# Pairwise products of a recommender head: left operands turned by multiples of 32 rows, so that one buffer of turned rows serves up to seven units

## The reference

```
score_k = exp((x @ w_a + b_a) @ w_b)           # two heads, (w1,b1,w2) and (w3,b3,w4)
q_k     = sum_n x[:, n] * softmax(masked score_k)[:, n]
h       = concat(q1, q2) @ w5 + b5             # 1024 x 300
f6      = h @ w6 + b6
iu, ju  = triu_indices(300, k=1)               # 44850 pairs
cross   = h[:, iu] * h[:, ju] * (v @ v.T)[iu, ju]
f7      = cross @ w7 + b7                      # w7 is 44850 x 300
out8    = concat(f6, f7) @ w8 + b8
out     = einsum('bu,bku->bk', out8, label)    # 1024 x 200
```

## Time and profile before

| | before |
|---|---|
| median of 3 runs | 2047.17 us (2040.95 to 2052.43) |
| profiled execution | 2043.87 us, span 2041.7 us |
| mean granted TensorE clock | 0.934 |
| TensorE busy | 1760.3 us, 86% |
| VectorE busy | 1455.3 us, 71% |
| ScalarE busy | 863.3 us, 42% |
| DMA moved | 629.75 MB, mean 308 GB/s |
| first unit starts | 164.3 us |
| phases 1, 2, 3 start (unit 0) | 588, 1033, 1482 us |
| last unit ends, tail starts | 1868.5 us |

### The profile page before, as it was taken

One profiled execution on the slowest core, in us unless ns is written; L12 is line 12 of the kernel. 1 busy time (PEld: TensorE's weight loads), 2 busy tenths in 40 slices (PEclk: granted clock), 3 DMA queues, 4 the chain that ended last, 5 costly groups with the idle time before them and its releaser, 6 DMA issues.

```text
span 2041.7 us, 23493 instructions
## 1 busy us (share of the span) xinstructions
PE 1760.3 (86%) x6820; PEld 1290.3 (63%) x6820; DVE 1455.3 (71%) x5499; ACT 863.3 (42%) x2413; POOL 22.7 (1%) x49
## 2 busy tenths in 40 slices
PE   3567999999999999999979999999889999998000
PEld 2345777777767777777657777777667777775000
DVE  8835645544147888988558898888536777773998
ACT  3525545545345564553345454553234444442000
POOL 0000000000000000000000000000000000000000
PEclk9788999999999999999989999999899999997555
DMA  6358566666566999999968999989869999995997
GB/s 223 126 165 315 190 234 238 219 242 237 193 240 241 359 354 379 354 382 405 350 246 303 361 340 392 348 340 389 273 252 356 404 406 408 409 391 178 392 395 310
DMA packets 121789, 629.75 MB, mean 308 GB/s; under 512 B 14136, under 2 KB 24921, under 8 KB 99133
## 3 DMA queue, kind: packets, MB, share of 16 engines
q1 hardware_dynamic: 93853, 408.04, 53.0%
q10 hardware_dynamic: 26208, 217.10, 28.0%
q0 software_dynamic: 1600, 3.10, 0.5%
HBM read 625.09 MB, written 3.10 MB: 308 GB/s over the span
## 4 chain that ended last, share of the span: by engine, by line
PE 79%; DVE 11%; DMA 6%; ACT 2%; issue 2%; POOL 0%; SPq 0%; DVEq 0%; ACTq 0%; POOLq 0%
PE bank L480 64%; PE bank L440 10%; DVE lring L775 8%; DMA sring<-hrows 3%; DMA lring<-in_label 2%; DMA wring<-in_w7p 2%; PE bank L452 1%; DVE junk L688 1%; ACT absjunk L546 1%; PE bank L462 1%; PE bank L490 1%; PE bank L488 1%; DVE cring L755 1%; ACT wring L608 1%; PE bank L432 0%
## 5 line engine op out<-in xcount | busy, mean ns | idle before, releaser
L480 PE MATMUL bank<-wring,cring 128*128 128x300 f32 x5616 | 1448.2, 419 | 38.9 <-DVE cring L755 38.2
L480 PEld LDWEIGHTS bank<-wring,cring 128*128 128x128 f32 x5616 | 1072.7, 192 | 398.7 <-DVE cring L755 40.1
L608 ACT ACTIVATE wring<-wring,gcol 128x300 f32<-128x300 f32 x1404 | 642.0, 532 | 786.6 <-PE bank L480 497.2
L755 DVE TENSOR_TENSOR cring<-hT,sring 128x1024 f32<-128x1024 f32 (+1 forms) x344 | 418.1, 1216 | 432.6 <-PE bank L480 386.6
L775 DVE SCALAR_TENSOR_TENSOR lring<-lring,out 128x300 f32<-128x300 f32 x1600 | 644.7, 465 | 29.9 <-DMA lring<-in_label 16.2
L688 DVE SCALAR_TENSOR_TENSOR junk<-xring,ubc 128x300 bf16<-128x300 f32 x800 | 328.1, 463 | 0.0
L440 PE MATMUL bank<-xring,wts 128*128 128x300 f32 x800 | 221.4, 429 | 64.9 <-DVE wts L733 64.9
L440 PEld LDWEIGHTS bank<-xring,wts 128*128 128x128 f32 x800 | 157.0, 197 | 119.2 <-issue 59.7
L546 ACT ACTIVATE absjunk<-xring 128x300 bf16<-128x300 f32 x400 | 174.9, 439 | 0.2
L775 DVE DVE_READ_ACCUMULATOR lring<-lring,out 128x1 f32 x1600 | 129.9, 81 | 0.0
L546 ACT ACTIVATION_READ_ACCUMULATOR absjunk<-xring 128x1 f32 x400 | 75.4, 189 | 0.0
(11 more groups left out here) (49 smaller groups left out, 182.9 us busy)
## 6 DMA issues: line engine op xcount, KB each, us to landing
lring<-in_label SPq DMA_DIRECT2D x320, 750.0 KB, 7.2
wring<-in_w7p ACTq DMA_DIRECT2D x168, 1200.0 KB, 8.0
sring<-hrows SPq DMA_DIRECT2D x172, 512.0 KB
xring<-in_x SPq DMA_DIRECT2D x80, 750.0 KB, 5.8
wring<-in_w7p ACTq DMA_DIRECT2D x8, 1050.0 KB, 8.1
sring<-hrows SPq DMA_DIRECT2D x16, 176.0 KB
sring<-hrows SPq DMA_DIRECT2D x16, 132.0 KB
sring<-hrows SPq DMA_DIRECT2D x8, 160.0 KB
```

The lines of the kernel that those rows point to most:

```text
L480: mm = pe.matmul(acc[(g * GB + b) % 4][:, 0:E], lhs, w, start=(t == 0), stop=(t == NT - 1))
L608: ins = nc.scalar.activation(w, w, ACT.Copy, scale=gcol[:, t:t + 1])
L755: nc.vector.tensor_tensor(cut(cring[:, k % CSLOTS]), in0, cut(sring[:, nb % SSLOTS]), ALU.mult).then_inc(c_ready, 1)
```

## The change

The pairs are dealt otherwise. A left operand may now also be a chunk turned by 32, 64 or 96 rows: A32, A64, B32, B64, B96, and C, the first 32 features of chunk C laid four times under one another. With lefts turned by multiples of 32 the rights need only turns of 0 to 31: 8 buffers of chunk A (NA), each read with the lefts A, B, A64, B32, B64, B96 and C (and the first also with A32 for one tile), 8 buffers of chunk B (NB), read with B, B64 and C (the first also with B32 for one tile), and 3 buffers (ND) of the last 12 features of C, read with A and B. The own units stay as they were. There are 91 units (three more have one or three tiles) and the same 351 tiles; 25 buffers are loaded in a phase, 19 of them of 512 KB in place of 43.

The six lefts lie in a new tile `lefts` (6 x 128 KB), loaded from `hrows` at the start of each phase by nine DMAs (`left_load`), between the phase's first and second `s_load` in SP's program; VectorE waits for them ahead of unit 2. `hrows` has a further region of the 12 features, 12 more small stores on GpSimd; the first two stores have a semaphore of their own, `a_stored`, and the phase's first buffer waits for those two alone, the lefts for the other 18 (`h_stored`). `sring` has 2 slots in place of 3. `w1T` no longer has a tile of its own. X_UNTIL is 62 in place of 68.

```diff
+NA, NB, ND = 8, 8, 3
+LEFTS = ("A32", "A64", "B32", "B64", "B96", "C")
...
-    for k in range(16):
+    for k in range(NA):
         first = 1 if k == 0 else 0
         units.append(("A", buf, first, QUAD - first))
         units.append(("B", buf, 0, QUAD))
+        if k == 0:
+            units.append(("A32", buf, 0, 1))
+        units.append(("A64", buf, first, QUAD - first))
+        for left in ("B32", "B64", "B96", "C"):
+            units.append((left, buf, 0, QUAD))
         buf += 1
-    for k in range(16):
-        units.append(("B", buf, 0, QUAD if k < 15 else QUAD - 1))
-        units.append(("A", buf, 0, QUAD))
+    for k in range(NB):
+        first = 1 if k == 0 else 0
+        units.append(("B", buf, first, QUAD - first))
+        if k == 0:
+            units.append(("B32", buf, 0, 1))
+        units.append(("B64", buf, first, QUAD - first))
+        units.append(("C", buf, 0, QUAD))
         buf += 1
-    for k in range(11):
+    for k in range(ND):
...
-    SSLOTS = 3
+    SSLOTS = 2
...
-    X_UNTIL = 68
+    X_UNTIL = 62
...
+            def left_load(g):
+
+                sp.wait_ge(h_stored, 16 * STORES * (g + 1))
+                for k, name in enumerate(LEFTS):
+                    dst, s = lefts[:, k, :], left_in
+                    if name == "C":
+                        for q in range(4):
+                            sp.dma_start(dst[32 * q:32 * q + 32], hrows[g % 2][C0:C0 + 32]).then_inc(s, 16)
+                    else:
+                        row = (A0 if name[0] == "A" else B0) + int(name[1:])
+                        sp.dma_start(dst, hrows[g % 2][row:row + P]).then_inc(s, 16)
...
                 if buf == 0:
-                    sp.wait_ge(h_stored, 16 * 8 * (g + 1))
+                    sp.wait_ge(a_stored, 16 * 2 * (g + 1))
...
                     sp.dma_start(slot, src).then_inc(s, 16)
+                    if buf == 0:
+                        left_load(g)
...
-                        done = [b for b in range(BUFS) if u == (2 * b + 1 if b < 43 else 86 + (b - 43) // 2)]
-                        for b in done:
+                        for b in [b for b in range(BUFS) if LAST_USE[b] == u]:
...
-                pool.dma_start(dst[A0:A0 + P], h[:, 0, :]).then_inc(h_stored, 16)
-                pool.dma_start(dst[A0 + P:A0 + A_ROWS], h[0:A_ROWS - P, 0, :]).then_inc(h_stored, 16)
+                pool.dma_start(dst[A0:A0 + P], h[:, 0, :]).then_inc(a_stored, 16)
+                pool.dma_start(dst[A0 + P:A0 + A_ROWS], h[0:A_ROWS - P, 0, :]).then_inc(a_stored, 16)
...
+                for r in range(0, D_ROWS, 12):
+                    n = min(12, D_ROWS - r)
+                    pool.dma_start(dst[D0 + r:D0 + r + n], h[32:32 + n, 2, :]).then_inc(h_stored, 16)
...
-                    in0 = hT[0:rows, g % 2, "AB".index(left), :].unsqueeze(1).to_broadcast([rows, n, L])
+                    one = hT[:, g % 2, "AB".index(left), :] if left in ("A", "B") else lefts[:, LEFTS.index(left), :]
+                    in0 = one.unsqueeze(1).to_broadcast([P, n, L])
+                if u == 2:
+                    dve.wait_ge(left_in, 16 * LEFT_LOADS * (g + 1))
```

More of the change, by code:

```diff
@@ L51, in tile_rows @@
     p = np.arange(P)
-    base = {"A": p, "B": P + p}
+    base = {"A": p, "B": P + p, "C": 2 * P + p % 32}
+    for name in LEFTS[:-1]:
+        base[name] = "AB".index(name[0]) * P + (p + int(name[1:])) % P
     units, _ = unit_table()
@@ L58, in tile_rows @@
                 break
-            if buf < 16:
+            if buf < NA:
                 right = (p + QUAD * buf + j) % P
-            elif buf < 32:
-                right = P + (p + QUAD * (buf - 16) + j + 1) % P
+            elif buf < NA + NB:
+                right = P + (p + QUAD * (buf - NA) + j) % P
             else:
-                right = 2 * P + (p + QUAD * (buf - 32) + j) % REST
+                right = 2 * P + 32 + (p + QUAD * (buf - NA - NB) + j) % 12
             tiles.append((base[left], right))
@@ L83 @@
 NU = len(UNITS)
+OWN = NA + NB + ND
+LAST_USE = [max(k for k, u in enumerate(UNITS) if u[1] == b or u[0] == "own" and u[1] == b - 1) for b in range(BUFS)]
 NT = sum(u[3] for u in UNITS)
@@ L135, in rec_kernel @@
         hT = sb("hT", [P, 2, NCH, L])
+        lefts = sb("lefts", [P, len(LEFTS), L])
         f6T = sb("f6T", [P, NCH, L])
@@ L160, in rec_kernel @@
         tick = sb("tick", [P, 1])
-        w1T = sb("w1T", [HID, 2, E + 1])
+        w1T = cring[0:HID, 0, 0:2 * E + 2].rearrange("p (k e) -> p k e", k=2)
         w2sb = sb("w2sb", [HID, 2])
@@ L165, in rec_kernel @@
         vl, vr, vp = (scratch[:, k * NT * VC:(k + 1) * NT * VC] for k in range(3))
-        A_ROWS, B_ROWS = P + 64, P + 65
-        C_ROWS = P + REST - 1
-        hrows = [nc.dram_tensor(f"hrows{k}", [A_ROWS + B_ROWS + C_ROWS, L], F32, kind="Internal").ap()
+        A_ROWS, B_ROWS = P + 64, P + 96
+        C_ROWS, D_ROWS = P + REST - 1, P + 11
+        hrows = [nc.dram_tensor(f"hrows{k}", [A_ROWS + B_ROWS + C_ROWS + D_ROWS, L], F32, kind="Internal").ap()
                  for k in range(2)]
         A0, B0, C0 = 0, A_ROWS, A_ROWS + B_ROWS
+        D0 = C0 + C_ROWS
+        STORES = 2 + -(-C_ROWS // REST) + -(-D_ROWS // 12)
+        LEFT_LOADS = 9
         bank = [ctx.enter_context(nc.psum_tensor(f"bank{k}", [P, 512], F32)) for k in range(8)]
@@ L186, in rec_kernel @@
         s_in = [sem(f"s_in{k}") for k in range(SSLOTS)]
+        left_in = sem("left_in")
         w7_in = [sem(f"w7_in{k}") for k in range(WSLOTS)]
@@ L200, in rec_kernel @@
         h_ready = sem("h_ready")
+        a_stored = sem("a_stored")
         h_stored = sem("h_stored")
@@ L305, in s_load @@
                 if buf == 0:
-                    sp.wait_ge(h_stored, 16 * 8 * (g + 1))
-                if buf < 43:
-                    row = (A0 + QUAD * buf if buf < 16 else B0 + QUAD * (buf - 16) + 1 if buf < 32
-                           else C0 + QUAD * (buf - 32))
+                    sp.wait_ge(a_stored, 16 * 2 * (g + 1))
+                if buf < OWN:
+                    row = (A0 + QUAD * buf if buf < NA else B0 + QUAD * (buf - NA) if buf < NA + NB
+                           else D0 + QUAD * (buf - NA - NB))
                     src = bass.AP(hrows[g % 2].tensor, row * L, [[L, P], [1, QUAD * L]])
                     sp.dma_start(slot, src).then_inc(s, 16)
+                    if buf == 0:
+                        left_load(g)
                     return
                 tiles = slot.rearrange("p (j l) -> p j l", l=L)
-                own, left = (buf - 43) // 2, (buf - 43) % 2
+                own, left = (buf - OWN) // 2, (buf - OWN) % 2
                 if own < 2:
@@ L758, in loads_of @@
             def loads_of(buf):
-                return 1 if buf < 43 else (5, 5, 3, 3, 5, 5)[buf - 43]
+                return 1 if buf < OWN else (5, 5, 3, 3, 5, 5)[buf - OWN]
             def landed(g, buf):
```

2 lines of the change are left out of this document (1 added, 1 removed).

## The result

The changed kernel takes 2060.78 us (median of 6 runs, 2054.85 to 2066.15) against 2045.66 us for the kernel before in the same comparison (6 runs): ratio 1.0062, interval [1.0040, 1.0084]. It is slower by 0.6%, 15 us. The profiled execution took 2061.34 us.

A forecast was written before the change was run, and what follows sets the result against it. TensorE sets the pace inside phases, and time is lost at the boundaries. Head -1, 0/1 +3, 1/2 +2.5, 2/3 +4 and end of phase 3 +2 sum to +10.5 on 2043.87, giving 2054 us, range 2020 to 2080.

The forecast's parts named there:

- 1/2: Boundary between phases 1 and 2: 16.9 us idle and 3 of slow matmuls, against 17.4 before, +2.5 us.
- Traffic inside a phase worth nothing: Inside phases: 49 MB less loaded, lefts give back 3; 28 us of DMA time a phase, covered by TensorE.
- The chain of own loads decides: End of each phase: with two slots each own load is issued only when the product before it is done.
- two-buffer link: Product 88 to 89 at a phase's end, load of two buffers: 9 us at 0/1, 11 at later boundaries.
- The first link: Product 87 to 88 at 1/2 and 2/3: 13.6 us, from 8 of backlog, 3.5 for the buffer, 2 for landing.
- 2/3: Boundary between phases 2 and 3: same links as at 1/2, 19.9 us lost against 16.0 before, +4 us.
- Slow matmuls behind the gaps: TensorE after the gaps at 1/2 and 2/3: records run slow, 3 us a boundary.
- 0/1: Boundary between phases 0 and 1, no labels loaded: the chain makes the next unit 0's product 2.8 us late, +3 us.
- End of phase 3: Links of 10, 11 and 5.4 us: 6.2 idle and 3.4 slow against 7.9 before, +2 us.
- Head: Program start: unit 0 at about 160 us, but unit 2 waits for the lefts until 172.5; -1 us.
- fast rival: Relief of DMA wins: full label ring, links at 1/2 and 2/3 as at 0/1; -30 us, 2014 us; chance 0.29.
- slow rival: Own-load chain as slow as the worst seen: links one and two at 18.5 us; +40 us, 2084 us; chance 0.18.

## Why the prediction was right, and where its terms were off

The forecast was 2054 us with 0.37 for slower and 2020 to 2080 as range; 2060.8 lies in it, and in the 2042 to 2066 of the likeliest case, on the upper side of both. The sum was +10.5 us; between the two profiled executions it was +17.8, and 3.7 of the 7.3 us missing are at 1/2 and 3.9 at the program's end. Point by point:

- *Traffic inside a phase worth nothing*: right as to the bytes saved. TensorE was busy inside the phases but for gaps for `w7` of 0.9 us in phase 1 and 1.9 us in phase 3, by the pairs with few tiles, which the prediction did not have.
- *The chain of own loads decides*: right in kind. The number of links and the absence of the `w7` gap came as said, and three gaps of the four, but not their sizes. Small links 4.7 and 4.4 us where I took 5.4 and 5.0, the two-buffer link 8.7 and 11.6 for 11.
- *The first link*: mis-sized, and with it the lead. I took 13.6 us and 2 us of lost lead; it was 19.5 us with 5.4 us of lead lost at 1/2, 14.6 us at 2/3. So the first gap was 11.3 us, not 1.9. I had worked out that the late stretch still asks for 448 GB/s of the 404 there are and is longer, and then priced the first link at 8 us of backlog at 404 GB/s and 5.5 for the buffer. DMA moved 5.4 MB in that link, where my backlog and the buffer are 3.7, and moved them at 279 GB/s, not 404; the 18.5 us of the kernel before, with 284, could have told me. With the own loads behind it the longer stretch costs 16 us in the kernel before and 11 to 13 in the changed grouping. That was the step that failed: the length of the stretch over which demand exceeds supply was noted, but not summed. The error shows only in part in the sum, and that is luck: product 88 ended 9.4 us later than forecast, but the three links behind it were 3.6 us shorter, and the forecast had 17 us of idle time at 1/2 where 18.7 came.
- *Slow matmuls behind the gaps*: I took 3 us a boundary; behind the three gaps they were 5.9 us at 1/2 and 7.4 at 2/3.
- *0/1*: +3 forecast, +3.3 measured, with links of 6.4, 7.5, 5.3 and 3.3 us. *End of phase 3*: +2 against +3.4, of which 1.9 are the gap for `w7` inside the phase. *Head*: -1 against -1.9, by two errors that cancel: unit 0 came at 163.5 us, not at about 160, since buffer 0 took 6.0 us and not 3.0, and the lefts were in at 168.7, so the gap ahead of unit 2 stayed away.
- *The program's end*: taken at nothing, +3.9. I had costed the 12 stores only in the head.
- *1/2*: +2.5 forecast, +6.2 measured, *2/3*: +4 and +3.0. For the kernel before I had counted 17.4 and 16.0 us there; with the small gaps and slow records that I left out it is some 20 and 19.

The fast rival fell: its premise, a full label ring when the own units come, did not hold. A label load took 10.9 us in the median from issue to landing already at 880 to 960 us, where the kernel before had 8.5, and between 860 and 1060 us VectorE waited 14.8 us for labels, before 11.5. Its rule (the Trainium skill, "DMA: Bandwidth & Descriptors", anatomy of one DMA: 2.0 us and bytes / 436e3, which the page gives for a DMA that GpSimd issues, while these are SyncE's) has the trace with it at 0/1, where the link of buffer 0 took 3.3 us, and against it behind the backlog, where the first link took 19.5. The slow rival's first link of 18.5 us came true at 1/2, but not its second.

What the kernel gained stayed hidden: with the old slots and X_UNTIL the regrouping is worth 14 us, most of it, by the trace, through the `w7` pair with few tiles at the phase's start. I had named that pair, but had not asked what it is worth without the chain. The slots (14 to 16 us) and X_UNTIL (11 to 13 us) took back more than that.

## What to carry to other kernels

Where a ring loses a slot, follow the last buffers before a boundary: each load that can only be issued when the product before it is done is a link at the full latency of its place, and the same chain cost 14 to 19 us of gaps behind a backlog and 4 to 9 where DMA had room. Sum what DMA is asked for over the whole stretch in which it exceeds what DMA gives, not per unit, before work is dealt into that stretch, and price a load in it by a link already measured there. And test a bundle part by part: here one part gained 14 us while two others lost 27, and the whole looked like a small loss.

## What the runs showed of the hardware that I had not expected

- The further small stores on GpSimd's queue lengthen the program's end by 3.9 us (5.7 to 9.6 us from the last store's issue to the end), in every kernel that had them; with two in place of twelve per group it is 6.8 us.
- With a load of 120 partitions under way that reads 12 rows ten times, DMA at full share moved 266 GB/s in a window where it moved 420 without it. With own loads of 64, 44 and 40 partitions under way it moved 302 at full share. What the two have in common was not tested.
- A load of 512 KB to `sring` took 6.0 us among small stores (156.40 us in the changed kernel) where it took 3.0 after the last of them.
